# An LSTM and its experts in one stage: the shares' products moved out of the second expert's steps, and an unread product in step 0 of each quarter

## The reference, cut to what matters

```python
def _L3_cond2_ref(x, h0, Wx, Wh, b):
    xW = jnp.einsum('ntd,dg->ntg', x, Wx) + b
    def step(carry, xw_t):
        prev_h, prev_c = carry
        a = xw_t + prev_h @ Wh
        i, f, o = (jax.nn.sigmoid(a[:, k * H:(k + 1) * H]) for k in range(3))
        g = jnp.tanh(a[:, 3 * H:])
        next_c = f * prev_c + i * g
        next_h = o * jnp.tanh(next_c)
        return ((next_h, next_c), next_h)
...
def _L3_ffn_ref(x, router_w, gate_w, gate_b, up_w, up_b, down_w, down_b):
    probs = jax.nn.softmax(xf @ router_w.T, axis=-1)
    topv, topi = jax.lax.top_k(probs, TOP_K)
    # probs kept at the two best, divided by their sum
    h = jax.nn.silu(xf @ gate + gate_b) * (xf @ up + up_b)
    expert_out = h @ down + down_b
    y = jnp.einsum('ne,ned->nd', probs, expert_out)
...
x = x + _L3_ffn_ref(_L3_cond2_ref(x, cond_1024, ...), ...)
```

## Time and profile before

| | us |
|---|---|
| median of 3 runs | 2799.14 |
| lowest, highest run | 2798.88, 2815.93 |
| the profiled execution | 2805.7 |
| its span, first to last instruction | 2803.9 |

### The profile page before, as it was taken

One profiled execution on the slowest core, in us unless ns is written; L12 is line 12 of the kernel. 1 busy time (PEld: TensorE's weight loads), 2 busy tenths in 40 slices (PEclk: granted clock), 3 DMA queues, 4 the chain that ended last, 5 costly groups with the idle time before them and its releaser, 6 DMA issues. The chain is left out here.

```text
span 2803.9 us, 91579 instructions
## 1 busy us (share of the span) xinstructions
PE 2402.1 (86%) x36869; PEld 1711.6 (61%) x36874; DVE 1650.7 (59%) x7006; ACT 1104.1 (39%) x4215; POOL 751.6 (27%) x1223
## 2 busy tenths in 40 slices
PE   5998888876389899779999999999768878999998
PEld 3555666665255546556667676765535556777774
DVE  3553555555545354347777777775356855666674
ACT  1332333332223343225556566554364423333332
POOL 1220000000111000117777777777253200000000
PEclk9997555555599999899999999999769955999999
DMA  2000000000100000124545455454100000000000
GB/s 98 3 3 2 2 2 2 2 2 2 41 2 3 2 1 0 69 45 99 120 107 116 106 116 111 109 111 115 53 9 2 2 2 2 2 2 2 2 3 16
DMA packets 110107, 104.24 MB, mean 37 GB/s; under 512 B 90496, under 2 KB 90496, under 8 KB 108800
## 3 DMA queue, kind: packets, MB, share of 16 engines
q1 hardware_dynamic: 109696, 98.50, 14.3%
HBM read 90.08 MB, written 8.39 MB: 35 GB/s over the span
## 5 line engine op out<-in xcount | busy, mean ns | idle before, releaser
L671 POOL TENSOR_TENSOR l2r_beta_s<-l2r_state,l2r_beta_f 128x256 f32<-128x256 f32 x512 | 370.0, 744 | 187.6 <-ACT l2r_state L574 184.2
L827 DVE TENSOR_TENSOR l2r_pre<-l2r_o_ps,l2r_beta_s 128x256 f32<-128x256 f32 x512 | 197.8, 421 | 84.7 <-PE l2r_o_ps L454 76.4
L574 ACT ACTIVATE l2r_state<-l2r_pre 128x256 f32<-128x256 f32 x512 | 189.9, 417 | 50.4 <-DVE l2r_pre L827 49.6
L140 PE MATMUL l0r_bank<-main_x,l0r_wx_half 128*128 128x32 f32 (+2 forms) x480 | 147.1, 406 | 60.5 <-ACT l0r_out_gate L196 59.9
L140 PEld LDWEIGHTS l0r_bank<-main_x,l0r_wx_half 128*128 128x128 f32 x480 | 115.9, 303 | 81.7 <-ACT l0r_out_gate L196 79.5
L1824 PEld LDWEIGHTS l3r_bank<-main_x,l3r_wx_half 128*128 128x128 f32 x480 | 96.7, 228 | 91.1 <-issue 46.2
L442 PE MATMUL l2r_d_ps<-l2r_state,l2r_kq 128*32 128x128 f32 x2056 | 147.9, 279 | 0.9 <-ACT l2r_state L574 0.7
L194 ACT ACTIVATE l0r_gates<-l0r_bank 128x24 f32<-128x24 f32 x256 | 48.6, 190 | 233.6 <-PE l0r_bank L152 233.6
L1963 ACT ACTIVATE l3r_gates<-l3r_bank 128x24 f32<-128x24 f32 x256 | 48.6, 190 | 228.0 <-PE l3r_bank L1836 227.8
L1807 POOL TENSOR_SCALAR main_y<-l3r_h_ring 128x128 f32<-128x128 f32 x16 | 8.4, 528 | 477.5 <-DVE l3r_h_ring L2117 477.5
L228 DVE SCALAR_TENSOR_TENSOR l0r_both<-l0r_gates 128x16 f32<-128x16 f32 x256 | 45.1, 176 | 149.8 <-ACT l0r_gates L194 149.8
(11 more groups left out here) (592 smaller groups left out, 7020.6 us busy)
## 6 DMA issues: line engine op xcount, KB each, us to landing
l2r_beta_f<-l2r_beta_store SPq DMA_DIRECT2D x256, 256.0 KB, 3.3
main_odd_layers<-in_l SPq DMA_DIRECT2D x1, 4826.5 KB, 14.5
main_odd_layers<-in_l SPq DMA_DIRECT2D x1, 3928.0 KB, 16.8
l2r_v_store<-l2r_v_part SPq DMA_DIRECT2D x32, 96.0 KB, 6.3
l2r_v_rows<-l2r_v_store SPq DMA_DIRECT2D x16, 192.0 KB, 4.9
main_decay<-in_decay SPq DMA_DIRECT2D x1, 3072.0 KB, 10.1
main_even_layers<-in_l SPq DMA_DIRECT2D x1, 2762.5 KB, 9.4
l2r_beta_store<-l2r_beta_tok SPq DMA_DIRECT2D x128, 16.0 KB, 1.6
```

The costliest lines, as they stand in the source:

```text
L140: nc.tensor.matmul(into, wx_half[:, g * P:(g + 1) * P], x_b[:, :, w * LW + lo:w * LW + hi].rearrange("p b t -> p t b"), start=False, stop= ...
L574: nc.scalar.activation(state[:, h * 2 * P:(h + 1) * 2 * P], pre[:, h * 2 * P:(h + 1) * 2 * P], ACT.Tanh).then_inc(state_ready[h], 1)
L671: nc.gpsimd.tensor_tensor(beta_s[:, half].rearrange("p (g r) -> p g r", g=HG), state[:, half].rearrange("p (g r) -> p g r", g=HG), beta_f[ ...
L827: nc.vector.tensor_tensor(pre[:, half].rearrange("p (c n) -> p c n", c=2), o_ps[:, 2 * h:2 * h + 2, 0:P], beta_s[:, half].rearrange("p (c ...
```

## The change

The three pieces 9, 10 and 11 now belong to no expert. The first expert stays in pieces 3 to 8, and experts two to eight begin three pieces later (the second in piece 12). The turn stands alone in piece 9, the bias product alone in piece 11, and step 10 gets an unread product. Everything behind moves by three: the last turn from piece 55 to 58, the addition to `x` from 56 to 59, the number of pieces from 57 to 60. The tuple of free steps is now 0, 1, 2, 7, 8, 10, 56, 57 and 59 to 63. In step 0 the unread product is queued before the logits, in the other steps behind the piece as before. In the first quarter step 58 has left the tuple, so the unread products there begin in step 59.

```diff
-        MOE_STEPS = 57
+        MOE_STEPS = 60
-        FREE_STEPS, FILL_FROM = (1, 2, 7, 8, 53, 54, 56, 57, 58, 59, 60, 61, 62, 63), T // NCHUNK - 6
-        FIRST_BLOCK, BLOCK = 3, 6
+        FREE_STEPS, FILL_FROM = (0, 1, 2, 7, 8, 10, 56, 57, 59, 60, 61, 62, 63), T // NCHUNK - 6
+        FIRST_BLOCK, BLOCK, SHARE_STEPS = 3, 6, 3
...
+        def block_at(q):
+
+            if FIRST_BLOCK + BLOCK <= q < FIRST_BLOCK + BLOCK + SHARE_STEPS:
+                return -1, 0
+            return divmod(q - FIRST_BLOCK - (SHARE_STEPS if q >= FIRST_BLOCK + BLOCK else 0), BLOCK)
...
-                    units = 2 * NEXP * (c - 1) + (0 if q < FIRST_BLOCK else 2 if q < FIRST_BLOCK + BLOCK else 2 * NEXP)
+                    units = 2 * NEXP * (c - 1) + (0 if q < FIRST_BLOCK else 2 if q < FIRST_BLOCK + BLOCK + SHARE_STEPS else 2 * NEXP)
...
-                    e, at = divmod(q - FIRST_BLOCK, BLOCK)
+                    e, at = block_at(q)
...
-                    if q == 55:
+                    if q == 58:
...
+                    fill = n >= FILL_FROM and n % QUARTER_STEPS in FREE_STEPS
+                    if fill and n % QUARTER_STEPS == 0:
+                        unread(n)
                     if experts_at(n):
                         experts(*experts_at(n))
-                    if n >= FILL_FROM and n % QUARTER_STEPS in FREE_STEPS:
+                    if fill and n % QUARTER_STEPS != 0:
                         unread(n)
...
-                    if q in (53, 54):
-                        add_expert(c, NEXP - 1, q - 53)
-                    if q == 56:
+                    if q in (56, 57):
+                        add_expert(c, NEXP - 1, q - 56)
+                    if q == 59:
```

## The result

| | before | after |
|---|---|---|
| median | 2804.5 us (20 runs) | 2815.5 us (20 runs) |
| lowest, highest | 2797.6, 2819.3 | 2808.1, 2821.2 |
| ratio, after to before | | 1.0030, 95% interval 1.0019 to 1.0040 |
| the profiled execution, its span | 2805.7, 2803.9 | 2819.1, 2816.8 |

The change makes the kernel 0.3% slower, 8.4 us by the ratio. That is within the 1% that was called "the same", and just inside the range of 2788 to 2817, but 13.5 us above the forecast of 2802 and outside the range of 2796 to 2808 that the forecast gave itself.

The account below looks back on a forecast made before the run. PE bounds the kernel wherever the chain leaves less room than a piece needs, with the clock deciding that need. Terms 2.0 - 2.3 - 4.7 + 3.9 + 3.3 = +2.2 us on median 2799.14 give 2801, stated as 2802; range 2788 to 2817.

Parts of the forecast that it names:

- Step 1: Step 0's unread product delays the logits, so step 1 grows by 0.65 us, +2.0 us in three quarters.
- Pieces 9 to 11: Steps 10 and 12 get shorter by 0.7 and 0.85 us, step 11 stays: -4.7 us in three quarters.
- Steps 13 on: Clock falls behind the bias product in all three quarters, one more 3.2 us piece of low clock each: +3.9 us.
- Rest of the quarter: Experts have the same pieces three steps later and the last addition still ends in time: 0.
- The tail: After the last quarter: bare wait for the copy, +0.9 us, and probable low clock, +2.4: together +3.3 us.
- term of steps 1 to 9: Start of each quarter at full clock: 4.9 us excess, 2.6 stay through falls in two of three quarters, 2.3 won.
- Quarter one loses one: First unread product of quarter one moves to step 59: costs nothing, though the clock may be up one step later.
- The rule that was weighed: Step 9: transposes don't count as PE-busy the same way, so a turn alone would be as thin as the logits.
- the rival built on it: Clock falls already in step 9, since a turn alone counts too little: +6 us in all, 2808 us; chance 0.10.
- low clock for longer: Falls behind the bias product and in the tail last three pieces more each: +13 us, 2812 us; chance 0.11.
- low clock past step 20: Sign in each quarter of longer low clock (2812 us, chance 0.11) or of locking low (2831 us, chance 0.02).
- The first rival: Both low stretches, at quarter starts and behind the bias product, go: -13.7 us, 2785 us; chance 0.17.

Follow-up runs that it names:

- padded kernel: The kernel before with the bias product made over 128 rows instead of 8, shares and biases padded with zeros: ratio 0.9968, median 2796.3 us.
- run with the old order: The changed kernel with the old order of pieces in the tail alone (gate and up between turn and bias product): ratio 1.0019.

## Why the prediction was right or wrong

It was right that the change is no change within 1% and that it leans to slower. It was right in most of the mechanism: steps 1 to 3 at full clock, low clock behind the bias product in all quarters, the wait and the low clock in the tail. It was too low by 5.5 us even on its own base (+2.9 forecast, +8.4 measured by the ratio), and that 2815.5 lies in the range owes something to the range's width. Five of its terms came out near their size, two did not. They are compared here between the two profiles, which differ by 9.3 us in the stage.

Step 1: 2.35, 2.35 and 2.35 us, +1.9 in all (forecast +2.0). Pieces 9 to 11: steps 10 to 12 took 4.3 us less (forecast -4.7), with step 10 at 1.72 and step 12 at 2.30 in two quarters. Steps 13 on: a fall in every quarter, +3.1 us (forecast +3.9). The padded kernel shows what this low clock costs in all: steps 13 to 18 lose 7.7 us to it in the kernel before, where the prediction put 7.0 on steps 13 to 16, from a full-clock step of 1.81 us; there the four take 6.95 us. Rest of the quarter: steps 19 to 63 take 243.0 us in the three quarters, before 242.8. Step 0 of quarter two, which the sum leaves out, is 0.4 us longer at low clock. The tail: +4.6 us (forecast +3.3, upper bound +6): right in its parts, a wait for the copy and 10.1 us of low clock (6.7 was assumed); the run with the old order shows that it comes with the order.

What failed first is the term of steps 1 to 9. "I put such a fall into two of three, at 3.2 x 0.41 = 1.3 us" was too small: without step 1's growth these steps took 0.7 us more than before, where 2.3 us less were forecast. The start was kept at full clock as hoped, but then the clock fell in step 4 or 6 of every quarter, for 3.2, 6.6 and 10.1 us. The kernel with step 0's product alone has three such falls. The price of a low stretch depends on what it covers: in quarter two it lies in step 5, which takes 2.69 us there as in the other two at full clock, and costs nearly nothing; in quarters three and four it covers steps 7 and 8, in four step 9 too, which have a product each (3.2, 2.8 and 2.8 us).

The other is "Quarter one loses one: its first is in step 59. At low clock that costs nothing without a product, but the clock may be up one step later." The second half was right and was priced at nothing. The clock rose at 2382.2 instead of 2368.6 us, four steps of the quarter had a product at low clock instead of about one and a half, and each of these takes 1.07 us more (2.80 against 1.73): +2.8 us. The two terms, 3.0 and 2.8 us, are most of the distance between +2.2 and the measured 9.3 us; the tail's excess of 1.3 us is the rest.

The rule that was weighed: the changed kernel has the turn alone in step 9 three times. In quarter two the clock is 1.00 from 2396.0 to 2409.4, over that step and the next two, and in quarter three from 2525.7 to 2532.3, over steps 9 to 11; in quarter four it was still low when step 9 began (until 2651.9). The Trainium skill (TensorE: Matmul & The Clock Gate, Part 4: PE-mode transpose) would have the fall there; the measurement disagrees, and the rival built on it is out.

Of the other rivals, low clock for longer (2812) came closest, with one quarter of 13.5 us behind the bias product and 10.1 us in the tail; low clock past step 20 did not occur. The first rival needed the bias product to hold the clock. It did not. With the padded one, which does, the changed kernel stands at 0.9995, not at the 0.995 of this rival: falls near the start of quarters three and four and the tail's loss (61.7 us) stay.

## What to carry to other kernels

Where TensorE's clock decides a stretch, list for each step what holds the clock and not only what keeps the engine busy: here a product with 8 rows took its full time and mostly didn't hold the clock, and padding its rows with zeros cost no time in the product (275 ns a record against 271). The filler product in step 0 moved the fall and did not remove it, in all three quarters, so look for the next thin step before counting the gain, and price the steps that the low clock will cover. When work is taken out of a shared step, read the same order where no other work surrounds it, here the tail.

## What the runs showed of the hardware that was not expected

In these runs the number of rows weighs most in whether a product holds the clock. Over 8 rows, 1.15 us of bias product let it fall in every quarter of before and of the changed kernel, and in 21 of 25 quarters over all profiles; over 128 rows, most of them zero, the clock fell behind it in none of eight quarters (in a ninth it was low already since step 6, and rose behind step 12). With the unread products over 8 rows PE stood at 0.50 for 61.3 us while busy all of it. A record takes 271 ns in the one form and 275 ns in the other, so the busy time of the profile can't tell them apart; the shape in its rows (8x128 against 128x128) can.
